# Another order of all engines within a turn of a gated delta-rule recurrence

## The reference, cut to what matters

```
q, k, v = silu(causal_conv(x @ W))            # 4 taps and a bias
k = k / max(norm(k), 1e-12)
v_old = S k_t
S = clip(alpha_t * S + beta_t * (v_t - alpha_t * v_old) k_t^T, -5, 5)
y_t = S q_t
```

## Time and profile before

| | us |
|---|---|
| median of 3 runs | 2020.57 |
| lowest and highest | 2012.62, 2022.43 |
| profiled execution, its own time | 2016.83 |
| its span, first to last instruction | 2015.3 |
| busy TensorE (model), VectorE | 1686.8 (84%), 1435.7 (71%) |
| busy GpSimd, ScalarE | 1064.8 (53%), 770.0 (38%) |
| mean granted TensorE clock | 0.91 |

### The profile page before, as it was taken

One profiled execution on the slowest core, in us unless ns is written; L12 is line 12 of the kernel. 1 busy time (PEld: TensorE's weight loads), 2 busy tenths in 40 slices (PEclk: granted clock), 3 DMA queues, 4 the chain that ended last, 5 costly groups with the idle time before them and its releaser, 6 DMA issues. The chain is left out here.

```text
span 2015.3 us, 59095 instructions
## 1 busy us (share of the span) xinstructions
PE 1686.8 (84%) x24752; PEld 1156.5 (57%) x24752; DVE 1435.7 (71%) x2156; ACT 770.0 (38%) x1314; POOL 1064.8 (53%) x1331
## 2 busy tenths in 40 slices
PE   7468889989889989889989988864889848999994
PEld 4235555555565565565555565643878845666662
DVE  5377798888888998888888897545787673444431
ACT  4335444444444543533533543212354232222221
POOL 0085576577567568558558558106453104555553
PEclk9688999899989999889889998786999869999997
DMA  3401212212312312222222212118333154444442
GB/s 121 94 18 33 73 44 57 81 51 57 81 54 54 79 55 59 68 55 61 66 55 55 64 45 54 44 53 301 118 117 122 42 213 94 87 83 86 84 87 40
DMA packets 89029, 156.52 MB, mean 78 GB/s; under 512 B 15676, under 2 KB 54084, under 8 KB 87564
## 3 DMA queue, kind: packets, MB, share of 16 engines
q1 hardware_dynamic: 72860, 124.76, 20.8%
q0 software_dynamic: 15904, 27.93, 7.2%
HBM read 112.53 MB, written 40.12 MB: 76 GB/s over the span
## 5 line engine op out<-in xcount | busy, mean ns | idle before, releaser
L1140 PE MATMUL d_ps<-hT,turn_shared 128*128 128x512 f32 x768 | 401.1, 635 | 19.2 <-DMA d_cw<-convp_in 10.3
L768 POOL TENSOR_TENSOR d_tmp<-turn_shared 128x31 f32<-128x31 f32 (+15 forms) x496 | 288.4, 581 | 71.1 <-DVE turn_shared L953 33.5
L773 POOL TENSOR_TENSOR turn_shared<-turn_shared,d_tmp 128x31 f32<-128x31 f32 (+15 forms) x496 | 288.2, 581 | 38.9
L837 DVE SCALAR_TENSOR_TENSOR turn_shared<-d_ps,d_cw,turn_shared 128x1023 f32<-128x1023 f32 (+2 forms) x192 | 242.6, 1265 | 16.5 <-ACT turn_shared L600 15.5
L649 ACT ACTIVATE d_U<-d_ps 128x128 f32<-128x128 f32 x256 | 70.8, 277 | 427.9 <-PE d_ps L1350 426.5
L1140 PEld LDWEIGHTS d_ps<-hT,turn_shared 128*128 128x128 f32 x768 | 129.4, 193 | 109.3 <-issue 76.4
L2195 POOL DMA_INDIRECT out<-m_yo,m_slot_i x71 | 113.1, 1592 | 132.2 <-DVE m_yo L2295 92.3
L2174 ACT ACTIVATE m_hm<-m_ps,m_b_tile 128x128 f32<-128x128 f32 x284 | 81.2, 368 | 226.2 <-PE m_ps L2343 226.2
L784 POOL TENSOR_TENSOR d_Z<-d_um,d_kmax 128x1024 f32<-128x1024 f32 x32 | 61.6, 1925 | 194.7 <-PE d_ps L1291 194.7
L868 DVE SCALAR_TENSOR_TENSOR d_S<-d_S,gamma_chunk,d_ps 128x64 f32<-128x64 f32 x448 | 104.3, 274 | 72.3 <-PE d_ps L1361 71.5
L2333 PE MATMUL m_ps<-m_w,m_xs 128*128 x284 | 138.5, 611 | 9.2 <-issue 7.9
(11 more groups left out here) (238 smaller groups left out, 3627.5 us busy)
## 6 DMA issues: line engine op xcount, KB each, us to landing
turn_shared<-steps_scratch SPq DMA_DIRECT2D x64, 256.0 KB
d_qg<-gamma_scratch SPq DMA_DIRECT2D x64, 256.0 KB, 4.7
y_scratch<-d_yT SPq DMA_DIRECT2D x256, 64.0 KB, 1.8
d_arow<-ab_scratch SPq DMA_DIRECT2D x128, 128.0 KB, 3.0
y<-y_scratch SPq DMA_DIRECT2D x8, 2048.0 KB, 8.2
m_w<-w_in SPq DMA_DIRECT2D x16, 512.0 KB, 10.2
turn_shared<-x_in SPq DMA_DIRECT2D x4, 1024.0 KB, 11.0
turn_shared<-x_by_half_in SPq DMA_DIRECT2D x8, 512.0 KB, 7.1
```

What stands on the lines that cost most here:

```text
L768: nc.gpsimd.tensor_tensor(tv, Tq[:, s + 1:, s].rearrange("p (r a) -> p r a", a=1).broadcast_to([P, left, known]), X[:, s, 0:known].rearran ...
L773: nc.gpsimd.tensor_tensor(X[:, s + 1:, 0:known], X[:, s + 1:, 0:known], tv, ALU.subtract).then_inc(s_sub, 1)
L837: nc.vector.scalar_tensor_tensor(out=dst[:, j + 1:], in0=src[:, 0:T - 1 - j], scalar=cw[:, u // BP % 2, n, 2 - j:3 - j], in1=dst[:, j + 1: ...
L1140: return nc.tensor.matmul(dst[:, g, :], w[:, m % 2, n, dc, :], hT[:, dc, at:at + G], start=(dc == 0), stop=(dc == DC - 1))
```

## The change

It reorders the lists of all engines within a turn. Every operation is still made by the same engine, with the same operands and sizes, except that the second half of `kq` uses the other pair of banks. `y_of_state` takes the head as a third argument, so that its two halves can stand apart. Where a pair of banks has another last reader in the new order, the wait is for that one.

On SP, `step_rows(un, 1)` comes ahead of `alpha_rows(tb, 1)`. On GpSimd, the new list is

(`ys` is `y_of_state`, `yu` is `y_of_u`, q 01 is `proj_q(u, 0, 1)`, an operation without a turn belongs to the one that it is made for.) The core of the diff:

```diff
-AT_KK, AT_KQ = (0, 1), (0, 0)
+AT_KK, AT_KQ = (0, 1), (0, 1)
...
                 if hf == 0:
                     pe.wait_ge(s_kt, 2 * u + 1)
                 else:
-                    pe.wait_ge(s_kt, 2 * u + 2)
+                    pe.wait_ge(s_vtap[1], 3 * u + 3)
...
-            def y_of_state(tc, k):
-                if k == 0:
-                    pe.wait_ge(s_A, 2 * tc + 2)
-                    pe.wait_ge(s_qg, tc + 1)
...
-                for h in range(2):
-                    if h == 1:
-                        pe.wait_ge(s_yq, 2 * (HC * tc + k) + 1)
...
+            def y_of_state(tc, k, h):
+                if h == 0:
+                    if k == 0:
+                        pe.wait_ge(s_A, 2 * tc + 2)
+                        pe.wait_ge(s_qg, tc + 1)
+                    if k % 2 == 0 and 4 * tc + k // 2:
+                        pe.wait_ge(s_ye, 4 * tc + k // 2)
+                    pe.wait_ge(s_y, HC * tc + k)
+                    pe.wait_ge(s_st, (NCW - 1) * tc + 2 * k + 1)
+                else:
+                    pe.wait_ge(s_yq, 2 * (HC * tc + k) + 1)
...
-                    if bound and c == 0:
-                        y_of_state(tb, 7)
...
-                    if bound and c == 0:
-                        y_of_u(tb, 7)
...
+                    if bound and c == 1:
+                        y_of_state(tb, 7, 0)
...
+                    if bound and c == 1:
+                        y_of_state(tb, 7, 1)
...
+                    if bound and c == 3:
+                        y_of_u(tb, 7)
```

More of the change, by code:

```diff
@@ L733, in _ @@
                         silu_q(u, 1)
+                        root(u)
                     if prep and c == 4:
@@ L737, in _ @@
                         first_v(u, 1)
-                    if prep and c == 5:
+                    if prep and c == 6:
                         keep_k(u, 1)
@@ L1029, in _ @@
                 for c in range(NCW):
+                    if bound and c == 0:
+                        update_max(tb, 2)
                     if chain and c == 0:
@@ L1486, in _ @@
                     if chain and c == 2:
-                        y_of_state(tc, 0)
                         seed_u(tc, 3)
-                        y_of_u(tc, 0)
+                    if bound and c == 3:
+                        y_of_u(tb, 7)
+                    if chain and c == 3:
+                        seed_u(tc, 4)
                     if prep and c == 3:
-                        proj_v(u, 1, 0)
                         proj_v(u, 1, 1)
                         proj_v(u, 1, 2)
-                    if chain and c == 3:
-                        y_of_state(tc, 1)
-                        seed_u(tc, 4)
                     if prep and c == 4:
@@ L1527, in _ @@
                     if chain and c == 10:
+                        y_of_u(tc, 3)
                         seed_u(tc, 11)
                     if chain and c == 11:
-                        y_of_state(tc, 4)
-                    if new_k and c == 11:
-                        proj_k(un, 1, 2)
-                        proj_k(un, 1, 3)
-                    if chain and c == 11:
+                        y_of_state(tc, 4, 1)
+                        y_of_u(tc, 4)
                         seed_u(tc, 12)
-                    if chain and c == 12:
-                        y_of_u(tc, 5)
+                        y_of_state(tc, 5, 0)
                     if prep and c == 12:
@@ L1543, in _ @@
                         z_turned(tb, 1)
-                    if chain and c == 13:
-                        y_of_state(tc, 6)
-                    if new_k and c == 13:
-                        kk(un, 0)
+                    if prep and c == 13:
+                        w_product(u, 0)
                     if chain and c == 13:
                         seed_u(tc, 14)
+                    if chain and c == 14:
+                        y_of_state(tc, 6, 0)
+                        y_of_state(tc, 6, 1)
                     if new_k and c == 14:
+                        kk(un, 0)
                         kk(un, 1)
-                        proj_q(un, 0, 0)
                     if chain and c == 14:
                         seed_u(tc, 15)
+                        y_of_u(tc, 6)
             pe.wait_ge(s_mx, 2 * TURNS + 3)
```

205 lines of the change are left out of this document (100 added, 105 removed).

## The result

The changed kernel takes 2085.55 us, median of four runs (2080.69 to 2092.63); the kernel before, run beside it, 2020.26 (2012.62 to 2022.43). The ratio is 1.0321, interval 1.029 to 1.0351: slower by 3.2%, some 65 us. The forecast was 2058 in a range of 1998 to 2092; it took the right side and fell 27 us short. One execution of a later run (one of ten of e5) took 2189.23 us at a mean clock of 0.725, far from its others; it is left out of that run's time.

The account below looks back on a forecast made before the run. VectorE and TensorE were both taken as near full, neither full. The order added 0, late loads 28 us and the clock 10 to the profiled 2016.83: 2055, or 2058 with the median 3.7 higher; range 1998 to 2092.

Parts of the forecast that it names:

- The late load: Steps 3 to 5: `gamma_rows` loads wait for the moved `y_of_u(tb, 7)`, delaying `decayed_q`; 2.0 us in 14 turns, 28 us.
- The second fall of the clock: Steps 4 to 5: TensorE idle 3.5 us of 6, so its clock may fall; 0.75 us in 14 turns, 10 us.
- The rest of the order: All five stretches of a turn: gains and losses cancel, 70.4 us at full clock, the same as before.
- the list: Each engine's new order set out by hand for a mid-run turn, with profiled durations at full clock; 70.4 us.
- 0.45 us of turn per us of low clock: Price of TensorE's low clock, read from two neighbouring turns of 71.80 and 75.30 us at clocks 0.98 and 0.93.
- The gain for TensorE: Parted heads save 1.4 us a turn, grouped projections 0.6: TensorE needs 2.0 less, which goes into waits.
- The quiet stretch at step 12 goes away: Rival: TensorE busy enough from step 11, losing 3.7 us of low clock a turn; -24 us, 1997; chance 0.18.
- The loads are hidden: Rival: last load lands within 3.1 us of issue, or `decayed_q` is late anyway; 2020 to 2030; chance 0.16.
- Low clock twice a turn: Rival: 10 us of low clock at step 12 and 6.8 at step 5 each turn; +83 us, 2103; chance 0.12.
- The table load: Step 4: 1.28 us now ahead of `silu_v`, since `root` moved to step 3; steps 4 to 7 11.3 against 9.4.

Follow-up runs that it names:

- e5: e1's order with three never-read 128x256 products a turn added on TensorE at steps 12 and 13: 2029.60 us, 1.0033 of before.
- e1: Changed kernel with product 7 of the turn before (both heads and `y_of_u`) put back to the late part of step 0: 2028.23 us, 1.0021 of before.
- e12: e1 with SP's `gamma_rows` loads also waiting for state update 3, so only the loads are late: 2090.13 us, 1.0341 of before.
- e3: Changed kernel with three never-read 128x512 products in TensorE's waits of step 4, ahead of `kq` and seed 5: 2062.98 us, 1.0214 of before.
- e7: Kernel before with `y_of_state` parted by heads and nothing else changed: 2024.89 us, 1.0019 of before.
- e8: e1 with `root`, and so its table load, moved back from step 3 to step 1: 2010.48 us, 0.994 of before.
- e4: Kernel before with `gamma_rows` also waiting until `keep_u` of step 3 is done, nothing else changed: 2062.14 us, 1.0216 of before.
- e9: e8 with GpSimd's `decay_k` 1 and 2 put ahead of `clear_x` again: 1989.21 us, 0.9854 of before.
- e6: Kernel before with three never-read products in step 12, ahead of the second cross product and the turned Z: 2031.42 us, 1.0039 of before.

## Why the prediction was right, and where it fell short

- **The late load: right in place, mechanism and nearly in size.** The forecast had the product end just behind state update 3, SP released then, the rows there 7.1 us later and `decayed_q` 4.0 us late. The rows show 7.16 and 4.03, in 14 turns; e1 and e12 show that this lateness is the loss. It also had the seed of step 5 wait for `kq` without the lateness, and 2.0 us longer with it. In e1 the seed does stand right behind `kq`, and in the change it comes 2.4 us later, inside the bounds of 0.3 to 2.5; e3 against e1 gives 2.3 by state update 7. That is 32 us in 14 turns for the forecast's 28.
- **The second fall of the clock: right in place, less than half its size.** This is the term that was mis-sized. It was taken at 0.75 us in bounds of 0 to 1.5, half of what 3.4 us of low clock would cost, with the argument that TensorE doesn't end those steps. In the change the falls that begin between state updates 3 and 5 last 7.9 us a turn, in each of the 13 turns, and they cost 2.0 us, above the upper bound: TensorE does end those steps then (in e3, at 1.00, steps 4 to 7 take 9.2, not 11.1). That is 28 us in 14 turns for the forecast's 10. Halving between "nothing" and "all" had no row behind it.
- **The sum.** Both terms come to 60 us against the 38 forecast. With the 0.4 us of step 2 they make up the 66 us between the profiled executions of e1 and the change; the medians of the two are 57 apart.
- **The rest of the order: zero, as forecast.** e1 is 1.0021 of before. The stretches came out near the list from 1 to 11 (14.5 against 14.0, 11.1 against 11.3, 18.1 against 18.3). The list was made at the full clock, and the low clock, which it took as unchanged at 3.7 us a turn, falls mostly from step 11 on: 11 to 14 took 14.5 for 12.1 and 14 to 1 16.2 for 14.7. In 14 to 1 about 1.0 us is the two operations that GpSimd stretches, which the list had at the durations of before; the sums agree only if the list was too long elsewhere by most of that, and to that extent the zero is luck.
- **Its readings.** The prediction's 0.45 us of turn per us of low clock comes from clocks rounded to 0.98 and 0.93; unrounded, those two turns have 3.4 and 10.2 us at the low clock, which gives 0.51. The 75.30 turn is 1.2 us over the mean of 74.1, not 0.9. The release of SP came 16 us later in the turn than before (26.6 us after state update 14 against 10.3), not "some 20". None of this moves the forecast by more than a few us.
- **The gain for TensorE: 2.0 us forecast, 2.1 measured** (e1), and the turn of e1 is not shorter for it, as forecast; how much of that is the clock's doing e7 leaves open. The waits of L1376 for itself went to one a turn:

```profile
PEld d_ps L1376 <- PE d_ps L1376: 2.7, 13, 0.2
PEld d_ps L1386 <- PE d_ps L1376: 5.7, 26, 0.6
PEld d_ps L1376 <- PE d_ps L1386: 3.2, 13, 0.2
```

  But `y_of_u`, now close behind, took three such waits a turn over, which the forecast had not: 8 became 4.
- **The rivals.** "The quiet stretch at step 12 goes away" did not come: the clock falls there in the change as before (0.53). "The loads are hidden" did not come either: `decayed_q` waited for them in 14 turns, and the last of four is there 7.1 us after SP's release. By the page "DMA: Bandwidth & Descriptors" of the Trainium skill (section "Anatomy of one DMA — SWDGE (gpsimd) path"), which measured another path, an estimate for one such load is 2.6 us. Here the last of the four took 5.2 us from issue to landing, so for loads that SP issues back to back the estimate is too low. "Low clock twice a turn" is nearest to what happened, and 2085.55 lies between the forecast and its 2103. Its fall at step 5 is there (7.9 us for 6.8 named), but those that begin at steps 11 and 12 did not grow (6.3 us a turn for 10 named; before had 7.4 there), and a us of the new one cost 0.25 us, not 0.45.
- **The table load: right.** The list had it on the path, in the 11.3 of steps 4 to 7, and e8 gains 18 us by taking it out; `kq` ends 1.4 us earlier after update 3 there (6.7 against 8.1).

## What to carry to other kernels

Before an instruction that frees a buffer is moved, look up who reloads that buffer and count from its end to the landing of the last transfer; here a product of 0.65 us, moved by three steps, made four loads late and cost 65 us. Lateness was not paid in proportion in this order: the slack swallows the first microseconds (a wait of 2.4 us cost 0.9), and once TensorE stood idle, its clock fell and the next stretch was paid too (4.1 cost 4.8). How much slack there is depends on the order: before, a wait of 2.9 cost 3.1 (e4). When a fall of the clock is likely and its price unknown, put the whole price into the range. When such a change loses, undo its moves one by one before giving it up: with product 7 early, the table load back and GpSimd's order turned, this one is 1.5% faster than before (1.1 to 1.8).

## What was not expected of the hardware

- A product of VectorE on `turn_shared` and `d_tmp`, 128x1024, took 1.23 us alone and 2.02 beside two products of GpSimd; the 128x32 one ahead of it 0.19 and 0.61. So a duration from a trace holds for what ran beside it, and the change moved GpSimd's order, which the forecast looked at for due times alone.
- TensorE stalls in the middle of a run of matmuls that wait for no semaphore. Here, in the changed kernel, for 1.75 us:

```profile
856.80 0.97 PE L1298 MATMUL d_ps<-turn_shared 32*32 32x32 f32 x92
...
858.34 0.44 PE L1386 MATMUL d_ps<-d_U,d_A 64*64 64x64 f32 x6
860.54 0.50 PE L1386 MATMUL d_ps<-d_U,d_A 64*64 64x64 f32 x9 [1.75 <-issue]
```

  In the DMA queues of 857 to 862 there is one packet of another kind than the rest, marked as instructions:

```profile
q1 hardware_dynamic: 357, 0.28, 24.0%
q8 instruction: 1, 0.02, 1.8%
```

  One such packet in 5 us would say little, since there are 140 between 240 and 1270 us. But all twelve stalls of TensorE over 1 us in that stretch, none of which a semaphore explains, have one that starts 0.1 to 1.7 us ahead of them, and each stall ends 1.3 to 1.6 us after that packet's end. The same holds for the 12 stalls of before and the 13 of e9 (1.2 to 1.6 us; 240 to 1200 us), while only 27 to 30% of all moments have such a packet starting in the 2 us ahead. So the stalls go with these packets. That TensorE waits for its own code there is inferred; no run tested it.
- More work can be less time: three products a turn in the hole of step 4, where TensorE stood idle, gave 23 us back (e3); three smaller ones at step 12 gave nothing, though they raised the clock as well (e5, e6).
